# The V product of a step placed behind the third instead of the second chunk of the next step's scores

## Chip, core and metric

One core of a Trainium2 chip runs the whole program. The metric is the device time of one execution in microseconds (us). Engines are named PE (TensorE, matmuls), ACT (ScalarE), DVE (VectorE), POOL (GpSimd) and SP (the queue that issues DMAs).

## What is computed

The input `x` is 4 x 2048 x 256 in fp32. First comes a full attention layer with 16 heads of width 16, then two local-attention and feed-forward layers. The change lies in the first attention, which is this part of the reference, cut to its core:

```python
x = x + attn(layernorm(x))
# attn: per batch (4) and head (16), L = 2048, hd = 16
scores = Q @ K.T / 4 + prior_lambda * gaussian_mask(L)   # 2048 x 2048
attn   = softmax(scores, axis=-1)
out    = attn @ V                                        # 2048 x 16
x = x + (out.transpose(...).reshape(B, L, 256) @ Wo.T + bo)
```

The mask is non-zero only near the diagonal (distance up to 59).

## The kernel before

There are 4 x 16 = 64 heads, and each head is worked in 16 steps of 128 rows, 1024 steps in all. A step `n` is head `n // 16`, key block `kb = n % 16`. The loop runs from `n = -20` to `n = 1024`, because two passes over the scores run 20 steps apart:

- **pass1** (L528) computes 128 queries x 2048 keys in four chunks of 512 columns, each of four matmuls into one of three PSUM banks (`a_b`). DVE takes the row maximum of each chunk, with a plain reduction (L811) or, where the mask reaches into the chunk, with a fused add-and-max (L809), followed by a short read of the accumulator. These maxima are turned into one more row of `q` (rows_T, L573, then ACT and a DMA) for pass2. The step that pass1 works on is 20 ahead of that of pass2.
- **pass2** (L543) computes the scores of 128 keys x 2048 queries, already shifted by the maximum, in four chunks into one of three other PSUM banks (`a_w`). Chunks near the diagonal get up to four small matmuls for the mask as well (L546). ACT takes the exponential of each chunk (L659) into `a_pr`, of which there are four pairs of chunks, so two steps' worth.
- **pv** (L565) is the V product: eight matmuls that multiply the exponentials of one whole step with V and accumulate into `a_po` over the 16 steps of a head. It belongs to the step before: in step `n` the loop calls `pv(n - 1)`. At the end of a head ACT copies `a_po` out (`a_osb`, L692), and the next head's first pv waits for that copy.

pass1 uses the lower 64 rows of the PE array, pass2 the upper 64, pv both halves. A bank is claimed by waiting for the reader of the chunk three before it in the same ring: `claim` waits on `s_free[i]`. In a step without other work pass2's chunk 2 therefore takes the bank that chunk 3 of the step before has left. pv waits for all four exponentials of its step, which is again chunk 3 of the step before.

Between the steps lie "units": projections of q and k (L471), values (L483), transposes of the input (L454), spreading of the softmax sums (L497) and the output projection (L513) of another batch. A table sets at which steps they are called, one per step at most, behind chunk 3. Each unit takes one bank of the `a_w` ring, and ACT copies it out (L620, L629, L641, L642, L649). DVE has side work in some steps as well (statistics for the layer norms, L712 and L784).

Each engine runs its own instruction list in order. The order on PE is the order in which the Python code calls the functions:

```python
for n in range(-LEAD, NS + 1):
    for c in range(4):
        pass1(n, c)
        pass2(n, c)
        if c == 1:
            pv(n - 1)
```

Of the kernel before, what the change touches and what calls it, by code (L numbers as in the profile page):

```python
# [235 lines left out]
def rows_at(n):  # L236

    return (n + LEAD) // W if (n + LEAD) % W == 1 and W < n + LEAD <= NS + 1 else 0
# [69 lines left out]
def attention(nc, S0, x1, a):  # L308
# [118 lines left out]
    def tensor(eng):  # L427
# [91 lines left out]
        def pass1(n, c):  # L519

            g, qb = divmod(n + LEAD, W)
            if g < NB * HA:
                s = g % 3
                bk, full = claim(("rows_of", g, qb, c))
                pe.wait_ge(s_pack[s], PACK * (g // 3 + 1))
                for r in range(4):
                    o = qb * 128 + 32 * r
                    m = eng.matmul(bk[32 * r:32 * r + 32, :], qp[s][0:DEEP, o:o + 32], kp[s][0:DEEP, c * 512:c * 512 + 512], start=True, stop=True)  # L528
                m.then_inc(full, 1)

        def pass2(n, c):

            if not 0 <= n < NS:
                return
            g, kb = divmod(n, W)
            s = g % 3
            pe.wait_ge(s_row[s], ROW * (g // 3 + 1))
            pe.wait_ge(s_setup, 3)
            bk, full = claim(("columns_of", n, c))
            near = [(q, w) for q in range(4) for w in windows(kb * 128 + 32 * q) if w[0] == c]  # L540
            for r in range(4):
                o = kb * 128 + 32 * r
                m = eng.matmul(bk[32 * r:32 * r + 32, :], kp[s][HALF:HALF + DEEP + 2, o:o + 32], qp[s][HALF:HALF + DEEP + 2, c * 512:c * 512 + 512],  # L543
                               start=True, stop=True, skip_group_check=True)
            for q, (_, c0, p0, n_) in near:
                m = eng.matmul(bk[32 * q:32 * q + 32, c0:c0 + n_], sel[HALF:128, :], mt[HALF:128, p0:p0 + n_], start=False, stop=True, skip_group_check=True)  # L546
            m.then_inc(full, 1)

        def pv(n):
            if not 0 <= n < NS:  # L550
                return
            g, kb = divmod(n, W)
            b, h = divmod(g, HA)
            i, k = slot["values", b, 3, 1]
            pe.wait_ge(s_free[i], k)
            pe.wait_ge(s_nh, 3 if b else 2)
            for c in range(4):
                i, k = slot["columns_of", n, c]
                pe.wait_ge(s_free[i], k)
            if kb == 0 and g:  # L560
                pe.wait_ge(s_osb, g)
            for half in range(2):
                rows = slice(HALF * half, HALF * half + HALF)
                for j in range(4):
                    m = eng.matmul(po[32 * j:32 * j + DA + 1, 512 * half:512 * half + 512], v[b % 2][rows, kb, h, :],  # L565
                                   pr[(2 * n + j // 2) % NP][rows, (j % 2) * 512:(j % 2) * 512 + 512], start=kb == 0, stop=kb == W - 1, skip_group_check=True)
            m.then_inc(s_pv, 1)

        def rows_T(what):
            bk, full = claim(what)  # L570
            pe.wait_ge(s_setup, 1)
            pe.wait_ge(s_pk, what[1] + 1)
            eng.transpose(bk.bitcast(F16)[0:32, 0:128], pk[:, :, :].rearrange("p a b -> p (a b)"), identh[:, :]).then_inc(full, 1)  # L573
# [14 lines left out]
        for n in range(-LEAD, NS + 1):  # L588
            for c in range(4):
                pass1(n, c)  # L590
                pass2(n, c)
                if c == 1:
                    pv(n - 1)
            if n in units:
                work[units[n][0]](units[n])
            if rows_at(n):
                rows_T(("rows", rows_at(n) - 1))
# [609 lines left out]
    with nc.Block() as block:  # L1207
        block.tensor(tensor)
        block.scalar(scalar)
        block.vector(vector)  # L1210
        block.gpsimd(gpsimd)
        block.sync(sync)
# [974 lines left out]
```

## Time and profile before

| | |
|---|---|
| median of 3 runs | 5791.14 us (5790.15 to 5794.63) |
| the profiled execution, time | 5793.11 us |
| the profiled execution, span | 5790.9 us |
| mean granted TensorE clock | 0.984 |
| PE busy | 5275.0 us (91%) |
| DVE busy | 4804.4 us (83%) |
| ACT busy | 4306.8 us (74%) |
| POOL busy | 2184.7 us (38%) |

The span is from the first to the last instruction. Shares are means over the whole program, of which the attention with the steps described above is the first 3155 us. PE's busy time is the time in which any matmul is in the array, also a lone one, so it is no measure of how full the array is.

### The profile page before, as it was taken

How to read it: one execution, taken by the hardware profiler on the slowest of the kernel's cores; microseconds unless marked ns; L12 is line 12 of the kernel's file. 1: busy time of each engine (PE TensorE's matmuls, PEld its weight loads, DVE VectorE, ACT ScalarE, POOL GpSimd, SP SyncE). 2: the span in 40 equal slices, each digit the busy share in tenths (PEclk: the TensorE clock that was granted, in tenths of full speed). 3: DMA queues.
4: the chain of work that ended last, by engine and by line, in shares of the span. 5: the costliest groups of instructions: out<-in, count | busy, mean ns of one | idle time of the engine just before them, and what ended most of it. 6: DMA issues, size and time to landing. Idle time of an engine off the chain costs nothing. (4 is left out here: it accounts for less than half of the span.)

```text
span 5790.9 us, 179656 instructions
## 1 busy us (share of the span) xinstructions
PE 5275.0 (91%) x75212; PEld 3174.8 (55%) x75340; DVE 4804.4 (83%) x9925; ACT 4306.8 (74%) x8522; POOL 2184.7 (38%) x1695
## 2 busy tenths in 40 slices
PE   8888888888888888888888999999999999999999
PEld 2333333333333333333332788888888888888787
DVE  5988899888899888999993888888676888888676
ACT  3888888888888888888886677777433677777333
POOL 2011102211013111031001789989111889988222
PEclk7999999999999999999997999999999999999999
DMA  2011101111111111111000454544100444555211
GB/s 83 22 31 37 36 24 35 46 38 35 29 29 44 40 38 33 31 44 46 25 22 12 113 116 111 115 113 112 50 12 6 112 113 113 115 116 113 58 55 48
DMA packets 262970, 343.32 MB, mean 59 GB/s; under 512 B 45664, under 2 KB 165520, under 8 KB 262160
## 3 DMA queue, kind: packets, MB, share of 16 engines
q1 hardware_dynamic: 262160, 331.84, 23.0%
q8 instruction: 592, 9.70, 0.7%
q14 instruction: 218, 1.79, 0.1%
HBM read 104.14 MB, written 33.55 MB: 24 GB/s over the span
## 5 line engine op out<-in xcount | busy, mean ns | idle before, releaser
L659 ACT ACTIVATE a_pr<-a_w,a_expscale 128x512 f32<-128x512 f32 x4096 | 2496.9, 688 | 283.1 <-PE a_w L543 177.9
L811 DVE TENSOR_REDUCE a_mx<-a_b 128x1 f32<-128x512 f32 x2688 | 1729.4, 685 | 235.2 <-PE a_b L528 231.1
L528 PE MATMUL a_b<-a_kp,a_qp 48*32 48x512 f16 x16384 | 1323.9, 384 | 199.3 <-DVE a_mx L809 99.0
L543 PE MATMUL a_w<-a_qp,a_kp 50*32 50x512 f16 x16384 | 1357.6, 385 | 32.3 <-ACT a_pr L659 25.4
L565 PE MATMUL a_po<-a_pr,a_v 64*17 64x512 f32 x16384 | 1143.5, 605 | 191.2 <-ACT a_pr L659 92.2
L528 PEld LDWEIGHTS a_b<-a_kp,a_qp 48*32 48x32 f16 x16384 | 430.9, 92 | 1211.5 <-issue 440.1
L809 DVE CUSTOM_DVE_ANT_0 a_junk<-a_b,a_gw 128x512 bf16<-128x512 f32 x1408 | 966.0, 686 | 144.7 <-PE a_b L528 101.3
L1709 POOL TENSOR_TENSOR l_p<-l_p,l_rc 128x512 f32<-128x512 f32 (+1 forms) x512 | 721.7, 1437 | 29.3 <-DVE l_rc L1607 29.2
L1497 ACT ACTIVATE l_p<-l_S,l_nm 128x256 f32<-128x256 f32 (+1 forms) x1024 | 470.8, 470 | 203.9 <-DVE l_nm L1599 203.9
L1351 PE MATMUL l_G<-l_wqkv,l_hT 128*128 128x512 f32 x2304 | 602.8, 406 | 9.5 <-DVE l_hT L1550 8.2
L543 PEld LDWEIGHTS a_w<-a_qp,a_kp 50*32 50x32 f16 x16384 | 441.6, 92 | 264.1 <-ACT a_pr L659 136.7
L1870 PE MATMUL f_F<-f_hT,f_w 128*128 128x512 f32 x2088 | 509.9, 398 | 1.9 <-DVE f_hT L2005 1.9
L1351 PEld LDWEIGHTS l_G<-l_wqkv,l_hT 128*128 128x128 f32 x2304 | 413.2, 188 | 113.7 <-issue 17.8
L565 PEld LDWEIGHTS a_po<-a_pr,a_v 64*17 64x17 f32 x16384 | 186.5, 92 | 475.6 <-ACT a_pr L659 359.0
L1870 PEld LDWEIGHTS f_F<-f_hT,f_w 128*128 128x128 f32 x2088 | 386.0, 188 | 88.1 <-DVE f_hT L2005 2.7
L954 POOL TENSOR_SCALAR a_r<-a_nm 128x16 f32<-128x16 f32 x64 | 16.5, 258 | 975.1 <-DVE a_nm L817 975.1
L1702 POOL TENSOR_TENSOR l_ri<-l_ss,l_nh 128x16 f32<-128x16 f32 x128 | 372.5, 2910 | 26.3 <-DVE l_ss L1575 20.0
L1948 ACT ACTIVATE f_u<-f_uf 128x512 fp32r<-128x512 f32 x160 | 101.2, 632 | 359.7 <-DVE f_uf L2017 359.7
L936 POOL TENSOR_TENSOR a_heads_sb<-a_osb 128x512 f32<-128x512 f32 x64 | 82.0, 1281 | 749.8 <-ACT a_osb L692 749.8
L1700 POOL TENSOR_TENSOR raw<-raw 128x1024 f32<-128x1024 f32 x128 | 305.5, 2386 | 135.1 <-DVE raw L1565 135.1
L1599 DVE TENSOR_REDUCE l_nm<-l_S 128x2 f32<-128x512 f32 (+1 forms) x512 | 338.4, 661 | 6.0 <-PE l_S L1380 5.5
L1505 ACT ACTIVATE l_pT<-l_R 128x512 f32<-128x512 f32 (+1 forms) x512 | 271.3, 582 | 82.8 <-PE l_R L1392 81.8
(258 smaller groups left out, 8873.0 us busy)
## 6 DMA issues: line engine op xcount, KB each, us to landing
l_qs<-l_qT SPq DMA_DIRECT2D x512, 128.0 KB, 2.3
l_kh<-l_kT SPq DMA_DIRECT2D x512, 128.0 KB, 2.4
l_kl<-l_kT SPq DMA_DIRECT2D x256, 128.0 KB, 2.4
a_qp<-q_parts SPq DMA_DIRECT2D x128, 128.0 KB, 2.8
a_kp<-k_parts SPq DMA_DIRECT2D x128, 128.0 KB, 3.1
l_tab<-in_rotary SPq DMA_DIRECT2D x128, 128.0 KB, 2.4
a_xc<-in_x SPq DMA_DIRECT2D x28, 512.0 KB, 3.8
q_parts<-raw SPq DMA_DIRECT2D x32, 256.0 KB, 2.1
```

Source lines behind the costliest of these rows:

```text
L528: m = eng.matmul(bk[32 * r:32 * r + 32, :], qp[s][0:DEEP, o:o + 32], kp[s][0:DEEP, c * 512:c * 512 + 512], start=True, stop=True)
L543: m = eng.matmul(bk[32 * r:32 * r + 32, :], kp[s][HALF:HALF + DEEP + 2, o:o + 32], qp[s][HALF:HALF + DEEP + 2, c * 512:c * 512 + 512], sta ...
L565: m = eng.matmul(po[32 * j:32 * j + DA + 1, 512 * half:512 * half + 512], v[b % 2][rows, kb, h, :], pr[(2 * n + j // 2) % NP][rows, (j % 2 ...
L659: eng.activation(pr[(2 * n + c // 2) % NP][:, o:o + 512], banks[i], ACT.Exp, scale=expscale[:, :]).then_inc(s_free[i], 1)
L809: t = eng.tensor_tensor_reduce(junk[:, :], banks[i], gw[:, o + WIDE0:o + WIDE0 + 512], 1.0, LOWEST, ALU.add, ALU.max, mx[g % 2][:, qb, c:c ...
L811: t = eng.tensor_reduce(mx[g % 2][:, qb, c:c + 1], banks[i], X, ALU.max)
L1351: m = eng.matmul(G[n % 2][:, :], hT[x][:, c * 128:c * 128 + 128], wq[z][:, c, n * 512:n * 512 + 512], start=i == 0, stop=i == 5)
L1497: y = eng.activation(dst, src, ACT.Exp, bias=nm[t % 2][:, hh:hh + 1], accum_out=sm[t % 2][:, hh:hh + 1])
L1599: eng.tensor_reduce(nm[t % 2][:, 2 * pair:2 * pair + 2], s[:, :].rearrange("p (h k) -> p h k", h=2) if w else z[:, :, 1, :], X, ALU.max, n ...
L1702: eng.tensor_tensor(ri[s][:, :], ss[s][:, :], nh[:, :], ALU.pow).then_inc(s_inv, 1)
L1709: eng.tensor_tensor(z, z, rc[t % 2][:, o:o + 2].unsqueeze(2).to_broadcast([128, 2, 256 if w else 128]), ALU.mult).then_inc(s_norm, 1)
L1870: m = eng.matmul(f[:, :], w1[x][:, c, col * 128:col * 128 + 128], hT[g % 2][z][:, c, :], start=n == 0, stop=n == 5)
```

## The change

One line is changed. In each step the eight matmuls of `pv(n - 1)` are called behind chunk 2 instead of behind chunk 1, on PE alone. Instruction lists of ACT, DVE, POOL and SP are the same as before.

```diff
             for c in range(4):
                 pass1(n, c)
                 pass2(n, c)
-                if c == 1:
+                if c == 2:
                     pv(n - 1)
```

In a step without a unit, this is PE's list before, from chunk 1 to chunk 2 (L528 is pass1, L543 pass2, L565 pv; `a_free0` to `a_free2` are the banks that DVE empties, `a_free3` to `a_free5` those that ACT empties):

```order
L528 MATMUL a_b<-a_kp,a_qp 32x512 [waits a_free1]
L528 MATMUL a_b<-a_kp,a_qp 32x512 x3
L543 MATMUL a_w<-a_qp,a_kp 32x512 [waits a_free5]
L543 MATMUL a_w<-a_qp,a_kp 32x512 x3
L565 MATMUL a_po<-a_pr,a_v 17x512 [waits a_free3]
L565 MATMUL a_po<-a_pr,a_v 17x512 x7
L528 MATMUL a_b<-a_kp,a_qp 32x512 [waits a_free2]
L528 MATMUL a_b<-a_kp,a_qp 32x512 x3
L543 MATMUL a_w<-a_qp,a_kp 32x512 x4
L546 MATMUL a_w<-a_mt,a_sel 32x150 x4
```

And this is the same place after, with chunk 3 behind it:

```order
L528 MATMUL a_b<-a_kp,a_qp 32x512 [waits a_free2]
L528 MATMUL a_b<-a_kp,a_qp 32x512 x3
L543 MATMUL a_w<-a_qp,a_kp 32x512 [waits a_free3]
L543 MATMUL a_w<-a_qp,a_kp 32x512 x3
L546 MATMUL a_w<-a_mt,a_sel 32x150 x4
L565 MATMUL a_po<-a_pr,a_v 17x512 x8
L528 MATMUL a_b<-a_kp,a_qp 32x512 [waits a_free0]
L528 MATMUL a_b<-a_kp,a_qp 32x512 x3
L543 MATMUL a_w<-a_qp,a_kp 32x512 [waits a_free4]
L543 MATMUL a_w<-a_qp,a_kp 32x512 x3
```

The wait for ACT's last exponential of the step before (`a_free3` here) stood on pv, with chunk 2 of both passes behind it; now it stands on pass2's chunk 2, pv follows without a wait of its own, and chunk 3 of both passes lies behind pv.

The second place is the step behind a unit, here the values (L483). Before:

```order
L483 MATMUL a_w<-a_wv,a_hT 32x256 x15
L528 MATMUL a_b<-a_kp,a_qp 32x512 [waits a_free0]
L528 MATMUL a_b<-a_kp,a_qp 32x512 x3
L543 MATMUL a_w<-a_qp,a_kp 32x512 [waits a_free5]
L543 MATMUL a_w<-a_qp,a_kp 32x512 x3
L528 MATMUL a_b<-a_kp,a_qp 32x512 [waits a_free1]
L528 MATMUL a_b<-a_kp,a_qp 32x512 x3
L543 MATMUL a_w<-a_qp,a_kp 32x512 [waits a_free3]
L543 MATMUL a_w<-a_qp,a_kp 32x512 x3
L546 MATMUL a_w<-a_mt,a_sel 32x150 x4
L565 MATMUL a_po<-a_pr,a_v 17x512 x8
```

After, from chunk 1's mask matmuls on:

```order
L546 MATMUL a_w<-a_mt,a_sel 32x150 x4
L528 MATMUL a_b<-a_kp,a_qp 32x512 [waits a_free2]
L528 MATMUL a_b<-a_kp,a_qp 32x512 x3
L543 MATMUL a_w<-a_qp,a_kp 32x512 [waits a_free4]
L543 MATMUL a_w<-a_qp,a_kp 32x512 x3
L565 MATMUL a_po<-a_pr,a_v 17x512 x8
```

Here the bank that pass2's chunk 2 claims is that of the unit, so pv now stands behind ACT's copy of the unit as well.

## Rows read from the trace of the kernel before

**Rows 1.** Busy time by stretch: the steps, the last 15, one short stretch.
```profile
131.20:3098.20 2967.00, 2554.13 (x56179) 948.22 (x56183) 2598.32 (x5689) 2622.13 (x4357) 419.43 (x505) 0.99 0.12 34
3098.20:3155.40 57.20, 54.74 (x537) 13.06 (x528) 0.00 (x0) 36.14 (x59) 0.00 (x0) 0.51 0.02 4
...
2188.00:2190.00 2.00, 2.00 (x40) 0.91 (x28) 0.54 (x1) 1.09 (x3) 2.00 (x2) 0.54 0.00 0
```
The columns are: stretch, its us, busy us of PE, PE's weight load, DVE, ACT and POOL (with instructions), granted TensorE clock, DMA share, GB/s.

**Rows 2.** Waits in 170 to 3110 us: us in total, times, longest.
```profile
ACT a_pr L659 <- PE a_w L543: 168.4, 562, 1.4
ACT a_pr L659 <- PE a_w L546: 94.6, 314, 1.3
...
ACT a_ob L649 <- PE a_w L513: 19.8, 24, 0.8
```

**Rows 3.** Page, costliest groups: busy us, mean ns of one | idle before.
```profile
L659 ACT ACTIVATE a_pr<-a_w,a_expscale 128x512 f32<-128x512 f32 x4096 | 2496.9, 688 | 283.1 <-PE a_w L543 177.9
```

**Rows 4.** Timeline of one plain step: start, us, engine, line, count, idle before.
```profile
1528.99 2.42 ACT L659 ACTIVATE a_pr<-a_w,a_expscale 128x512 f32<-128x512 f32 x4 [0.27 <-PE a_w L543]
...
1530.31 1.08 PE L565 MATMUL a_po<-a_pr,a_v 64*17 64x512 f32 x16
1531.18 0.40 PE L528 MATMUL a_b<-a_kp,a_qp 48*32 48x512 f16 x4
1531.21 0.40 PE L543 MATMUL a_w<-a_qp,a_kp 50*32 50x512 f16 x4
...
1531.62 0.69 DVE L809 CUSTOM_DVE_ANT_0 a_junk<-a_b,a_gw 128x512 bf16<-128x512 f32 x1 [0.19 <-PE a_b L528]
...
1531.68 2.42 ACT L659 ACTIVATE a_pr<-a_w,a_expscale 128x512 f32<-128x512 f32 x4 [0.27 <-PE a_w L543]
...
1532.23 1.88 DVE L811 TENSOR_REDUCE a_mx<-a_b 128x1 f32<-128x512 f32 x3
```

**Rows 5.** Timeline where pass2 stands directly ahead of pv.
```profile
1510.33 0.40 PE L543 MATMUL a_w<-a_qp,a_kp 50*32 50x512 f16 x4 [0.17 <-ACT a_pr L659]
1510.35 1.24 PE L565 MATMUL a_po<-a_pr,a_v 64*17 64x512 f32 x16
...
1511.22 0.40 PE L528 MATMUL a_b<-a_kp,a_qp 48*32 48x512 f16 x4
1511.42 0.39 PE L543 MATMUL a_w<-a_qp,a_kp 50*32 50x512 f16 x4
```

**Rows 6.** Timeline of DVE: two masked chunks, one behind the other.
```profile
1581.34 0.69 DVE L809 CUSTOM_DVE_ANT_0 a_junk<-a_b,a_gw 128x512 bf16<-128x512 f32 x1 [0.19 <-PE a_b L528]
...
1582.18 0.69 DVE L809 CUSTOM_DVE_ANT_0 a_junk<-a_b,a_gw 128x512 bf16<-128x512 f32 x1
```

**Rows 7.** Timeline of ACT around a long unit: an output projection, a k projection.
```profile
1701.86 2.42 ACT L659 ACTIVATE a_pr<-a_w,a_expscale 128x512 f32<-128x512 f32 x4 [0.27 <-PE a_w L543]
...
1707.11 3.62 ACT L659 ACTIVATE a_pr<-a_w,a_expscale 128x512 f32<-128x512 f32 x6
...
2147.02 2.42 ACT L659 ACTIVATE a_pr<-a_w,a_expscale 128x512 f32<-128x512 f32 x4 [0.27 <-PE a_w L543]
...
2153.11 3.57 ACT L659 ACTIVATE a_pr<-a_w,a_expscale 128x512 f32<-128x512 f32 x6
```

**Rows 8.** Timeline of ACT and DVE at a head's end.
```profile
1561.59 1.26 ACT L659 ACTIVATE a_pr<-a_w,a_expscale 128x512 f32<-128x512 f32 x2 [0.27 <-PE a_w L543]
1562.74 1.02 ACT L692 ACTIVATE a_osb<-a_po 128x1024 f32<-128x1024 f32 x1
...
1565.22 1.89 DVE L811 TENSOR_REDUCE a_mx<-a_b 128x1 f32<-128x512 f32 x3 [1.20 <-PE a_b L528]
...
1607.08 1.02 ACT L692 ACTIVATE a_osb<-a_po 128x1024 f32<-128x1024 f32 x1
```

**Rows 9.** Timeline of ACT in the last head.
```profile
3109.41 2.42 ACT L659 ACTIVATE a_pr<-a_w,a_expscale 128x512 f32<-128x512 f32 x4 [1.30 <-PE a_w L543]
```

## Prediction, made before the changed kernel ran

> **What bounds the kernel now.** I read first the busy time by stretch, to see what the change can reach. The steps run from 131 to 3098 us; in these 2967 us DVE is busy 2598 and ACT 2622, so neither is full, and the granted clock is 0.99, the 2.4 GHz level. The last 15 steps, without pass1, run at 0.51, the 1.2 GHz level [rows 1]. Behind 3155 us nothing is touched.
>
> Then the waits. ACT waits 562 + 314 = 876 times for a pass2 chunk, 263 us, about 0.30 us each [rows 2]. The timeline of one step shows where. ACT starts four exponentials at 1528.99, and the next four at 1531.68: a period of 2.69. Four in a row take 2.42, one alone takes 0.69 [rows 3], so they start (2.42 - 0.69)/3 = 0.58 apart and ACT alone could do a step in 2.31. The four in a row are chunks 2 and 3 of step n-1, then chunks 0 and 1 of step n. Call T the end of chunk 3's exponential: 1528.99 + 0.58 + 0.69 = 1530.26. pv starts at T + 0.05, pass1's chunk 2 at T + 0.92, pass2's at T + 0.95, and the exponential of chunk 2 at T + 1.42, that is 0.47 after its matmuls. ACT had run out of chunks 0 and 1 before that [rows 4]. So pv's 0.87 us lies between the end of one step's exponentials and the third chunk of the next. DVE waits for the same pv: it gets chunk 2 at 1531.62, 0.44 after the matmuls, having waited 0.19 [rows 4].
>
> **What the change does to a plain step.** Nothing is added or removed, the eight matmuls move behind chunk 2, so the cost is all in who waits for whom.
>
> pass2's chunk 2 now starts at T + 0.05, where pv started, and its exponential can run at T + 0.52, while ACT wants it only at T - 0.11 + 2 x 0.58 = T + 1.05. Hidden, with 0.5 to spare. pv comes behind it. Where a row transposition has shifted the ring, the old kernel already has pass2 ahead of pv: pass2 at 1510.33, pv at 1510.35, then pass1 at 1511.22 and pass2 at 1511.42 [rows 5]. So pv starts its lower half at once and its upper half about 0.2 later; pass1's chunk 3 comes 0.89, pass2's 1.09 behind the first pass2. Taken over: pass1's chunk 3 at T + 0.94, pass2's at T + 1.14, exponential at T + 1.61. ACT wants chunk 3 at T + 1.62. It just fits, so PE and ACT together could turn a step in about 2.31 instead of 2.69. With mask matmuls in chunk 2 or 3 I add up to 0.1.
>
> The Trainium skill bears on this spot (TensorE: Matmul & The Clock Gate, section The mechanism): matmuls start and end in program order, and weights are loaded beside running matmuls only where the row group differs. Read strictly, pv's upper half could not be prepared under pass2's chunk 2, and all of pv would lie 0.2 later; the row agrees for the upper half and not for the lower. By the strict reading chunk 3 would be 0.2 late in each plain step, the first rival below.
>
> Next DVE. Three plain reductions in a row take 1.88, so (1.88 - 0.69)/2 = 0.60 from one to the next, and a masked chunk is 0.61 ahead of the next start (1531.62 to 1532.23) [rows 4]. A masked one behind a masked one starts 0.84 later [rows 6]. The mask reaches 22 of a head's 64 chunks, and 7 of them stand ahead of another masked one, counted from the code. A head costs DVE 42 x 0.60 + 15 x 0.61 + 7 x 0.84 = 40.2 us, or 2.51 a step. **DVE becomes the bound**: 2.51 against ACT's 2.31. PE does not hold it back: from one chunk-3 reduction to the next the path through pass1's chunk 2, pv and pass1's chunk 3 is 0.69 + 0.05 + 0.22 + 0.87 + 0.44 = 2.27, under 2.41. Today a plain head takes 1607.08 - 1562.74 = 44.34 [rows 8].
>
> **What is not won.** (a) At a head's end the first pv waits for ACT's copy of a_po. ACT starts chunk 3 at 1561.59 + 0.58 = 1562.17; the copy ends at 1563.76, so pv is 0.9 later than otherwise, and today DVE idles 1.20 there [rows 8]. Afterwards chunk 2 is ahead of it, and of that idle I work out 2.95 - 2.41 = 0.54 if DVE comes to it without lag (pv at 1.64, chunk 3's matmuls at 2.51, its reduction at 2.95, counted from ACT's start of chunk 3), about 0.5: 62 x 0.5 = 31 us. (b) Long units. There are four rows of 24 waits (the one shown, and the like for values, q and k projections), 96 in all [rows 2]. With PE busy on the unit, two steps take, from chunk 3's start to chunk 3's start, (1707.11 + 1.73) - (1701.86 + 0.58) = 6.40 for 48 of them and (2153.11 + 1.73) - (2147.02 + 0.58) = 7.24 for the 48 projections [rows 7]. PE and ACT set these, not the place of pv: pv moves behind ACT's copy of the unit, but chunk 3 is still ready when ACT gets there. I cost them at no change. DVE idles in them by 6.40 - 5.03 and 7.24 - 5.03, together 66 + 106 = 172 us, which also hides its statistics. (c) Mask matmuls and small misfits between the engines: 0.25 a head, 15 us.
>
> **The sum.** pass1 runs in 1004 steps, 62.75 heads, from 131 to about 3084 (3098 less five steps of 2.69). Afterwards: 62.75 x 40.2 = 2523, + 172 + 31 + 15 = 2741 us, against 2953: 212 less. The five steps left at full clock win 0.38 each (2 us). The last 15: a step is now 2.42 + 1.30 = 3.72 [rows 9]; pv at half clock (1.74) still bounds them, and putting one pass2 chunk (0.43) ahead and one exponential less behind saves 0.58 - 0.43 = 0.15 each (2 us). In all 216. As a second way: 22 plain heads win 44.34 - 40.9 = 3.4 each (75), and the 876 - 352 = 524 other waits about 0.24 each (126): 201. I take 209, between the two. The profiled execution took 5793.1, 2 over the median, so 5584 by it and 5582 by the median.
>
> **Rivals.**
> - The forecast, DVE becomes the bound and about 209 us go: 0.66, its own range 5545 to 5630.
> - The wait moves to chunk 3. It fits by 0.01 only. If all of pv runs behind pass2's chunk 2 and the masks, chunk 3 is 0.2 to 0.3 late, ACT's step is 2.5 to 2.6, and added to DVE's uneven load some 0.12 of each of 812 plain steps is lost: 5582 + 97 = 5680. For it: no slack. Against: the overlap in [rows 5]. 0.19.
> - DVE's load fits better between the waits than I think (its reductions slide into the long units), so nearly all of ACT's 263 us go: 5791 - 263 = 5528. 0.07.
> - No change, because another wait steps in at once in full: the row of maxima or the loads of q and k, whose times in us stay while the steps shrink. They would have to take all of the 0.17 a step. Nothing on PE waits for them now. 0.03.
> - Slower: the clock. PE must stay at 2.4 GHz in the steps. It fell to 0.54 at 2188, where PE had waited for a copy of a_po [rows 1], and in the last head a step at 0.51 takes 3.72 [rows 9]. A plain step in that state costs at least 3.72 - 2.51 = 1.2 more, so from 209/1.2 = 174 such steps on the kernel is slower; with 300 it would be 5582 + 360 = 5942. Against: PE's pauses get shorter and one chunk more is worked in the pause at a head's end. 0.05. The Trainium skill describes this case (TensorE: Matmul & The Clock Gate, A second HAM failure mode: psum-queue depth-cycling): a PE that pauses briefly between groups while it goes round its PSUM banks can swing between the two levels. The row of the steps, 0.99 with the same pauses, does not show it.
>
> **How the numbers follow.** Predicted is the likeliest, 5582. The range runs from 5535 to 5685: it takes in the forecast's own and most of the second, and ends just above the third. About 0.2% (12 us) is what a measurement tells from no change. Faster: 0.66 + 0.19 + 0.07 = 0.92; same 0.03; slower 0.05.
>
> **What would show it.** ACT's 263 us of waits for L543 and L546 fall under 120; what remains for it stands on chunk 3. DVE's waits fall from 369 idle to about 180, and it is over 93% busy in the steps. A plain head takes about 40.9. PE's waits for DVE grow. Pairs of steps with a long unit stay at 6.4 and 7.2. Wrong it would be if ACT waits 0.2 at chunk 3 in each step, if DVE's spacing of 0.60 grows when PE and ACT are fuller, or if the clock of the steps drops under 0.97.

## The result

| | before | changed |
|---|---|---|
| median | 5790.65 us (5783.14 to 5794.63, 4 runs) | 5565.25 us (5561.30 to 5567.32, 4 runs) |
| profiled execution | 5793.11 us | 5561.30 us |
| span | 5790.9 us | 5559.5 us |
| mean granted TensorE clock | 0.984 | 0.991 |

The changed kernel takes 0.9611 of the time of the kernel before (95% interval 0.9595 to 0.9628): 225 us less by the medians. The forecast was 5582 us, range 5535 to 5685.

Where the time went is read from ACT's copies of `a_po` (L692), one at the end of each of the 64 heads. The profiled spans differ by 231.4 us:

| stretch | before | changed | less |
|---|---|---|---|
| up to the copy of the first head | 178.1 | 171.9 | 6.2 |
| 19 heads with no unit in them ("plain heads" below), each | 44.35 | 40.43 | 3.92 (74.5 in all) |
| the 43 others up to the 63rd copy | 2075.0 | 1944.6 | 130.4 |
| the last head | 58.66 | 37.24 | 21.4 |
| all behind | 2636.5 | 2637.6 | -1.1 |

Three more heads have no unit in them either; they win 3.5 to 4.4 us each and are counted with the 43, of which 40 have units.

These are the stretches and the waits in the trace of the changed kernel. First, the busy time of the steps and of the last head (columns as in [rows 1]):

```profile
131.20:2884.60 2753.40, 2495.86 (x56119) 944.75 (x56103) 2537.21 (x5684) 2580.77 (x4349) 417.56 (x503) 1.00 0.13 36
2885.00:2922.00 37.00, 32.73 (x556) 9.60 (x552) 0.00 (x0) 35.68 (x62) 1.28 (x1) 1.00 0.03 6
```

DVE is idle for 216 us of the steps now, against 369 before [rows 1]. The last head ran at a clock of 0.51 before; now it is at 1.00, the 2.4 GHz level, and ACT is busy in nearly all of it.

The clock changed in the steps ahead of it as well. Between the first copy of `a_po` and the last head the trace of the kernel before has nine short stretches at the lower level, of which that at 2188 [rows 1] is one. Eight of the nine begin within 2 us behind the start of a head's copy, during or just behind PE's pause for it. The changed kernel has one such stretch, at 327, and none at a head's end. Here are two more of the kernel before, and the one of the changed kernel:

```profile
608.00:610.00 2.00, 2.00 (x39) 0.68 (x20) 0.72 (x2) 1.08 (x3) 1.74 (x2) 0.50 0.04 11
1373.00:1375.00 2.00, 2.00 (x40) 0.62 (x28) 0.23 (x1) 0.67 (x2) 1.80 (x2) 0.50 0.01 2
```

```profile
327.00:329.00 2.00, 2.00 (x37) 0.49 (x25) 1.36 (x4) 0.89 (x3) 2.00 (x3) 0.50 0.00 0
```

Next, the waits in 170 to 2870 us (us in total, times, longest):

```profile
ACT a_pr L659 <- PE a_w L543: 31.5, 130, 0.8
ACT a_v L629 <- PE a_w L483: 28.2, 24, 1.2
ACT a_tmp L641 <- PE a_w L471: 28.1, 24, 1.2
ACT a_ob L649 <- PE a_w L513: 28.0, 24, 1.2
ACT raw L641 <- PE a_w L471: 27.2, 24, 1.2
ACT a_pr L659 <- PE a_w L546: 12.1, 39, 1.7
...
DVE a_mx L811 <- PE a_b L528: 102.2, 131, 1.5
DVE a_junk L809 <- PE a_b L528: 35.4, 36, 1.7
```

ACT's 876 waits for a chunk of pass2, 263 us [rows 2], are 169 waits and 44 us. They stood on chunk 2 (873 of the 876); all 169 that are left stand on chunk 3. Its waits for the long units have grown, from 19.8 us in 24 waits [rows 2] to about 28 in each of the four groups. The timeline of plain steps (columns as in [rows 4]) shows the new order of things:

```profile
798.94 7.23 ACT L659 ACTIVATE a_pr<-a_w,a_expscale 128x512 f32<-128x512 f32 x12 [0.23 <-PE a_w L543]
799.02 0.08 DVE L809 DVE_READ_ACCUMULATOR2_ANT a_mx<- 128x1 f32 x1
799.02 1.88 DVE L811 TENSOR_REDUCE a_mx<-a_b 128x1 f32<-128x512 f32 x3
...
799.76 0.40 PE L528 MATMUL a_b<-a_kp,a_qp 48*32 48x512 f16 x4
799.77 0.40 PE L543 MATMUL a_w<-a_qp,a_kp 50*32 50x512 f16 x4
799.99 1.04 PE L565 MATMUL a_po<-a_pr,a_v 64*17 64x512 f32 x16
800.82 0.68 DVE L809 CUSTOM_DVE_ANT_0 a_junk<-a_b,a_gw 128x512 bf16<-128x512 f32 x1
800.85 0.39 PE L528 MATMUL a_b<-a_kp,a_qp 48*32 48x512 f16 x4
800.86 0.39 PE L543 MATMUL a_w<-a_qp,a_kp 50*32 50x512 f16 x4
...
801.42 1.88 DVE L811 TENSOR_REDUCE a_mx<-a_b 128x1 f32<-128x512 f32 x3
```

DVE goes from 799.02 to 801.42 without a gap, a step of 2.40. Chunk 2 of both passes (799.76) now stands ahead of pv (799.99), chunk 3 (800.85) behind it, and ACT works through twelve exponentials with no wait. What is left of DVE's idle time in a plain head is at the head's end, where [rows 8] had 1.20:

```profile
826.96 1.02 ACT L692 ACTIVATE a_osb<-a_po 128x1024 f32<-128x1024 f32 x1
...
829.43 0.69 DVE L811 TENSOR_REDUCE a_mx<-a_b 128x1 f32<-128x512 f32 x1 [0.24 <-PE a_b L528]
```

### The profile page after: what moved, and what is told of

It reads as the page before. It is cut to its first block and busy times, and to the rows that moved or that the text cites. A ratio compares the mean times of both kernels' runs of the same rounds, so it can differ in the third digit from the quotient of the medians.

```text
span 5559.5 us, 179608 instructions
## 1 busy us (share of the span) xinstructions
PE 5193.5 (93%) x75212; PEld 3169.5 (57%) x75340; DVE 4744.1 (85%) x9925; ACT 4269.2 (77%) x8522; POOL 2185.2 (39%) x1695
## 5 line engine op out<-in xcount | busy, mean ns | idle before, releaser
L659 ACT ACTIVATE a_pr<-a_w,a_expscale 128x512 f32<-128x512 f32 x4096 | 2455.6, 698 | 59.6 <-PE a_w L543 33.7
L811 DVE TENSOR_REDUCE a_mx<-a_b 128x1 f32<-128x512 f32 x2688 | 1705.3, 683 | 124.1 <-PE a_b L528 117.3
L528 PE MATMUL a_b<-a_kp,a_qp 48*32 48x512 f16 x16384 | 1424.1, 383 | 197.8 <-DVE a_mx L809 92.4
L543 PE MATMUL a_w<-a_qp,a_kp 50*32 50x512 f16 x16384 | 1459.4, 383 | 51.7 <-ACT raw L642 39.0
L565 PE MATMUL a_po<-a_pr,a_v 64*17 64x512 f32 x16384 | 1165.1, 591 | 21.5 <-ACT a_osb L692 20.6
L528 PEld LDWEIGHTS a_b<-a_kp,a_qp 48*32 48x32 f16 x16384 | 403.2, 90 | 1272.4 <-DVE a_mx L811 627.0
L543 PEld LDWEIGHTS a_w<-a_qp,a_kp 50*32 50x32 f16 x16384 | 413.8, 90 | 284.5 <-ACT a_pr L659 117.7
L565 PEld LDWEIGHTS a_po<-a_pr,a_v 64*17 64x17 f32 x16384 | 282.2, 93 | 96.8 <-ACT a_osb L692 38.8
```

The costliest lines, as they stand in the source:

```text
L659: eng.activation(pr[(2 * n + c // 2) % NP][:, o:o + 512], banks[i], ACT.Exp, scale=expscale[:, :]).then_inc(s_free[i], 1)
L811: t = eng.tensor_reduce(mx[g % 2][:, qb, c:c + 1], banks[i], X, ALU.max)
```

## The experiments

**Theory**: the V product lay between ACT's last exponential of a step and the third chunk of the next; behind chunk 2 it is covered, and DVE's work on the maxima is the bound. **Rivals**: ACT, or PE's chain through chunk 3, is the new bound; and, for the last head, the low clock is given and only a shorter chain counts. All medians below stand beside runs of the kernel before on the same chip, whose medians lie at 5789 to 5792 us. The changed kernel itself was not run again beside them, so a difference from its 5565 us can be off by some 2 us.

### Two scratch tiles for the masked maxima

A masked chunk on DVE writes a scratch tile `junk` and waits for the masked chunk before it. With two tiles it waits for the one before that, which is long done. The second tile lies on constants that are no longer used; the lines that declare it are left out here.

```diff
-                if junk_of:
-                    dve.wait_ge(*junk_of.pop())
+                if len(junk_of) > 1:
+                    dve.wait_ge(*junk_of[-2])
                 junk_of.append((s_free[i], k))
-                t = eng.tensor_tensor_reduce(junk[:, :], ...
+                t = eng.tensor_tensor_reduce(junks[len(junk_of) % 2], ...
```

On the changed kernel:

> The changed kernel, with two scratch tiles for the masked maxima instead of one, so that a masked chunk behind a masked one need not wait 0.23 us for it. If DVE bounds the changed kernel, a head's floor on DVE falls by 7 x 0.23 = 1.6 us; ACT and PE then come near (38.1 and about 39 a head), so I expect plain heads at 39.0 to 39.6 instead of 40.4 and 5565 - 55 = 5510 (5490 to 5530). Rival: ACT or the PE chain through chunk 3 is the bound (ACT's exponentials run 0.607 apart without a gap); then nothing changes, 5565 within 8.

5506.07 us (5504.17 to 5508.52), ratio 0.9506 (0.9493 to 0.9519) to the kernel before: 59 us below the changed kernel. Plain heads take 39.28 us. The timeline of DVE in this kernel shows the second masked chunk 0.61 behind the first, where [rows 6] has 0.84:

```profile
781.08 0.68 DVE L810 CUSTOM_DVE_ANT_0 a_junk<-a_b,a_gw 128x512 bf16<-128x512 f32 x1
781.69 0.09 DVE L810 DVE_READ_ACCUMULATOR2_ANT a_mx<- 128x1 f32 x1
781.69 0.69 DVE L810 CUSTOM_DVE_ANT_0 a_ones_gt<-a_b,a_gw 128x512 bf16<-128x512 f32 x1
782.30 0.09 DVE L810 DVE_READ_ACCUMULATOR2_ANT a_mx<- 128x1 f32 x1
```

On the kernel before:

> The kernel before, with the same two scratch tiles. If the V product behind chunk 1 bounds it, DVE's pairs lie beside that wait, plain heads stay at 44.35 and the time within 8 us of 5791. If DVE had a share in the old bound, it is faster by up to 1.6 us a head, 5700.

5789.47 us (10 runs, 5786.08 to 5793.62), ratio 0.9997 (0.9988 to 1.0006), plain heads 44.36. The same edit on DVE is worth nothing while pv stands behind chunk 1 and 59 us once it stands behind chunk 2. So DVE was not the bound before and is after. The plain heads win 1.15 us each of the 1.6 by which DVE's floor fell: from 40.43 to 39.28, with the floor now at 40.2 - 1.6 = 38.6. What takes the remaining 0.4 was not traced.

### Pass2's chunk 2 worked twice

The four matmuls of pass2's chunk 2 are issued twice, the second time over the first, which adds 0.22 us of PE time in each step and leaves the output as it is.

```diff
-            for r in range(4):
+            for r in list(range(4)) * (2 if c == 2 else 1):
```

> The kernel before, with pass2's four matmuls of chunk 2 issued twice in each step (0.22 us of PE time more, same output). If chunk 2 behind the V product is on the chain that sets ACT's pace, each of some 812 plain steps grows by 0.22: 5791 + 178 = 5969. If PE has slack there, nothing changes.

5982.90 us (two runs), ratio 1.0333 (1.0313 to 1.0354): 192 us more, and plain heads at 47.5 instead of 44.35, 0.20 a step. Chunk 2 behind pv was on the chain.

> The changed kernel, with the same doubling. Chunk 2 itself is wanted 0.5 us after it is ready, but the V product and chunk 3 stand behind it. My forecast has ACT's chunk 3 just in time for a step of 2.31 and DVE at 2.51, so of 0.22 us the first 0.2 should be swallowed: 5565 + 10 to + 60 (5575 to 5625). If chunk 3 were already on the chain, all of it comes through: 5565 + 178 = 5743. If PE had ample slack: 5565.

5676.96 us (5669.03 to 5683.12), ratio 0.9804 (0.9789 to 0.9819): 112 us over the changed kernel, a miss. The plain heads did what was expected: 41.62 against 40.43, 0.07 a step out of 0.22. The remainder lies in the 43 other heads, 2026.8 against 1944.6, 82 us or 1.9 a head. I had left out the steps with a long unit and behind one, where PE is the bound. From one chunk 3 on ACT to the one two steps on, the 96 pairs of such steps grew by 0.30 to 0.42 us out of 0.44 added, 32 us in all; each other step by 0.07, 812 x 0.07 = 57. Together 89 of 112; the remainder was not traced. Chunk 2 itself is off the chain, and by this run PE has some 0.15 us of slack in a plain step and little around long units.

### The V product behind chunk 3

```diff
-                if c == 2:
+                if c == 3:
                     pv(n - 1)
```

> The V product behind chunk 3. If DVE bounds the changed kernel, the plain heads stay at 40.2 to 40.4; the rest of DVE's idle time at a head's end (0.24) goes, as chunk 3 no longer waits for ACT's copy, and pairs with a long unit may get back 0.1 to 0.3: 5545 to 5565. Rival: the V product now stands ahead of the next step's chunks 0 and 1 and ACT waits there: over 5600.

5632.09 us (5621.51 to 5642.62), ratio 0.9727 (0.9711 to 0.9744), slower than behind chunk 2. The plain heads stay at 40.57, which was expected. The loss lies in the other 43 heads, 2000.2 against 1944.6. Its waits on ACT:

```profile
ACT a_tmp L641 <- PE a_w L471: 40.7, 24, 1.8
ACT a_v L629 <- PE a_w L483: 40.3, 24, 2.0
ACT raw L641 <- PE a_w L471: 38.3, 24, 1.8
ACT a_ob L649 <- PE a_w L513: 36.1, 24, 1.5
```

The unit stands behind pv on PE, and the later pv is, the longer ACT waits for the unit: 0.84, 1.16 and 1.62 us for the three places. In two of the four runs the clock of the last head fell as well (the mean clock reads 0.985 and 0.986 in the slower two, 0.990 and 0.991 in the faster).

### The place of the V product around long units

First with the old place in the steps behind a long unit (`long` is `units[n - 1][0] in HOLDS`, and then `c == 1`):

> The changed kernel, but in the 96 or so steps behind a long unit the V product stays behind chunk 1. I costed these steps at no change; then this kernel is at 5565 within 8. If the move costs time there (the pairs of steps read 6.5 and 7.55 in the trace of the changed kernel against 6.4 and 7.24 before), it is up to 48 x 0.11 + 48 x 0.31 = 20 us faster: 5545. If the move gains there: slower than 5573.

5567.19 us (5564.92 to 5569.00), ratio 0.9616 (0.9600 to 0.9632): no difference. Then, on the kernel with two scratch tiles, with the old place in the steps that hold the unit:

```diff
+                long = n in units and units[n][0] in HOLDS
-                if c == 2:
+                if c == (1 if long else 2):
                     pv(n - 1)
```

> The kernel with two scratch tiles (5506 us), and the V product back behind chunk 1 in the steps that hold a long unit themselves. In the changed kernel ACT waits 1.15 us for each of the 96 long units instead of 0.84, 31 us more in all. If that comes from chunk 3 and the unit standing behind the V product in the unit's own step, the waits go back towards 0.84 and the time falls by 10 to 30 us: 5476 to 5496. If PE is the bound in these steps wherever the V product stands, nothing changes: 5506 within 8. If DVE loses there what it gains (chunk 2 is late again): slower, 5515 to 5530.

5507.88 us (5506.62 to 5508.98), ratio 0.9509 (0.9493 to 0.9525) against 0.9506: no difference. The waits of this kernel say why:

```profile
ACT a_pr L661 <- PE a_w L547: 22.4, 76, 1.7
ACT a_v L631 <- PE a_w L484: 20.9, 24, 1.1
...
ACT a_pr L661 <- PE a_w L544: 16.7, 59, 0.8
```

ACT's waits for the units are back at 0.84 each, and its waits for chunks of pass2 have grown from 14 to 39 us in exchange. The wait was moved, not removed. A pair of steps with a long unit, from chunk 3 to chunk 3 on ACT, takes 6.42 us (output projections), 6.59 (values) and 7.44 (projections) in the kernel with two scratch tiles, and 6.47, 6.59 and 7.44 here: PE's work sets the pair, wherever pv stands in it.

### The last head and its clock

The kernel before, with the new place only in the last 15 steps (from the third of the last head on):

```diff
-                if c == 1:
+                if c == (2 if n > NS - W + 1 else 1):
                     pv(n - 1)
```

> The kernel before, with the V product behind chunk 2 only in the last head (15 steps). My forecast costed this part at 2 us, because it took the 1.2 GHz level of that head as given. The trace of the changed kernel shows the head at 1.00 and 21 us shorter. If the place of the V product in these steps alone keeps the clock up, this kernel has a granted clock near 1.00 in the last head and is about 21 us faster than the kernel before (5770). Rival: the clock is kept up by what went before (fuller heads); then the head stays at 0.5 and the gain is 2 us (5789).

5792.53 us (11 runs, 5783.61 to 5794.73), ratio 0.9998 (0.9989 to 1.0006). The first theory fell. In its last head:

```profile
3096.50:3100.00 3.50, 2.03 (x38) 0.75 (x36) 0.00 (x0) 3.17 (x6) 1.27 (x1) 1.00 0.00 0
3100.00:3104.00 4.00, 3.82 (x50) 1.16 (x54) 0.00 (x0) 2.88 (x6) 0.00 (x0) 0.51 0.18 39
3104.00:3120.00 16.00, 16.00 (x174) 4.42 (x168) 0.00 (x0) 11.24 (x19) 0.00 (x0) 0.50 0.00 1
```

And the other way round (`1 if n > NS - W + 1 else 2`):

> The changed kernel, with the V product back behind chunk 1 in the last head only. By the first theory the clock falls to 0.5 there and the time is 19 to 21 us over that of the changed kernel (about 5585). By the rival (what went before decides) the clock stays and only the plain loss of 15 x 0.36 = 5 us comes back (5570).

5571.32 us (5566.99 to 5574.11), ratio 0.9620 (0.9607 to 0.9633). The clock stays at 1.00 with pv at the old place, and the head takes 42.23, 5 us more than with the new one. So the same last 15 steps run at either level, and what decides lies ahead of them. Just ahead is the step in which pv of the new head waits for the copy of `a_po`. PE's pause there is 1.19 us in the kernel before, and 0.52 in this experiment, as in the changed kernel, since a chunk is worked first. The rows are one of the kernel before and one of this experiment:

```profile
3096.91 1.08 PE L565 MATMUL a_po<-a_pr,a_v 64*17 64x512 f32 x16 [1.19 <-ACT a_osb L692]
```

```profile
2887.09 1.08 PE L565 MATMUL a_po<-a_pr,a_v 64*17 64x512 f32 x16 [0.52 <-ACT a_osb L692]
```

So that single step was changed alone, in both directions (`n == NS - W + 1` in place of `n > NS - W + 1`):

> The kernel before, with the V product behind chunk 2 in one single step: the second of the last head, in which PE pauses for ACT's copy of a_po. The place in the 14 steps behind it did not matter (clock 0.50 with the new place there, 1.00 with the old one). If this one step with its pause decides whether the clock falls, the last head is 42.2 us long at a clock of 1.00 and the kernel 16 us faster than before: 5775. Rival: what matters lies further back (how full the heads with pass1 are), then the last head stays at 58 us and the time at 5791.

> The changed kernel, with the V product behind chunk 1 in that one step only. If the step decides: the clock falls to 0.50 and the last head takes 56 us instead of 37, 5565 + 19 = 5584. Rival, further back: 37.5 us and 5565.

Both came out mixed. The kernel before with the new place in that step: 5770 to 5795 us, five of ten runs at 5770 to 5779 with a mean clock of 0.989 or 0.990, five at 5784 to 5795 with 0.983 to 0.986; ratio 0.9986 (0.9975 to 0.9997). The changed kernel with the old place there: 5564.22 and 5564.51 us at 0.991 and 0.990, 5581.76 and 5586.66 at 0.986 and 0.985; ratio 0.9625 (0.9605 to 0.9645). The profiled execution is one in which it fell:

```profile
2888.59 1.08 PE L565 MATMUL a_po<-a_pr,a_v 64*17 64x512 f32 x16 [1.19 <-ACT a_osb L692]
```

```profile
2887.00:2891.00 4.00, 2.53 (x44) 0.85 (x40) 0.00 (x0) 3.67 (x6) 1.28 (x1) 1.00 0.00 0
2891.00:2895.00 4.00, 3.82 (x50) 1.22 (x54) 0.00 (x0) 2.88 (x6) 0.00 (x0) 0.54 0.16 35
```

In these runs the one step moves the odds to about half, in either kernel (five of ten and two of four, a small count); it does not decide alone. The last try fills PE instead: the kernel before, with pass2's chunks 0 and 1 worked twice in the last head (`2 if c < 2 and n >= NS - W else 1`).

> The kernel before, with pass2's matmuls of chunks 0 and 1 issued twice in the last head (16 steps, same output), which fills PE where it would idle. If a fuller PE in the last head keeps the clock up, the head takes about 43 us at 1.00: 5775. If the clock falls all the same, the doubled matmuls cost at half clock: 58.7 + up to 16 x 0.86 = 72 us, 5791 to 5805.

5797.05 us (10 runs, 5776.79 to 5804.38), ratio 1.0003 (0.9992 to 1.0015). In seven runs the clock fell (0.983 to 0.985) and the doubled matmuls were paid at half clock; three, at 0.988 or 0.989, took 5777 to 5782. More work in the last head helps some runs and not most.

One earlier run bears on this too: the kernel before with pass2's chunk 2 worked twice in every step. Its pv is at the old place, and its pause ahead of the last head is 1.19 us as in the kernel before. Yet the clock stays up through the last head, which takes 46.60 us; its two runs, 5982.99 and 5982.81 us, agree. These are its pause and its last head:

```profile
3297.77 1.08 PE L565 MATMUL a_po<-a_pr,a_v 64*17 64x512 f32 x16 [1.19 <-ACT a_osb L692]
```

```profile
3297.00:3341.00 44.00, 35.54 (x600) 11.78 (x600) 0.00 (x0) 36.81 (x61) 1.29 (x1) 1.00 0.02 5
```

So a pause of 1.19 us does not always bring the fall. The 62 earlier heads' ends of the kernel before say the same: PE's pause there is 1.00 to 1.19 us, and 1.86 at three of them, and the eight short falls include these three and five with 1.19. In the changed kernel no such pause is over 0.52 us, and there is no fall.

## Why the prediction was right, and where it was not

**What bounded the kernel.** Right. Doubling chunk 2 cost the kernel before 0.20 us a step and the changed one 0.07 in its plain heads.

**Chunk 3 just in time.** Right. In the last head, where DVE has nothing to do, 60 exponentials run without a wait. This is the row of ACT in the changed kernel:

```profile
2885.59 35.02 ACT L659 ACTIVATE a_pr<-a_w,a_expscale 128x512 f32<-128x512 f32 x60
```

That is (35.02 - 0.69)/59 = 0.58 each, 2.33 a step against the 2.31 worked out. There is no pass1 in that head. Where pass1 runs too, ACT reaches the same pace when it has been held up, as behind the end of a head at 1587 in the changed kernel, (4.73 - 0.69)/7 = 0.58:

```profile
1587.70 4.73 ACT L659 ACTIVATE a_pr<-a_w,a_expscale 128x512 f32<-128x512 f32 x8
```

The strict reading, in which all of pv starts 0.2 late and chunk 3 with it, came half true. In the last head pv starts with pass2's chunk 2, and the next chunk of pass2 comes 1.08 behind:

```profile
2888.11 0.40 PE L543 MATMUL a_w<-a_qp,a_kp 50*32 50x512 f16 x4 [0.18 <-ACT a_pr L659]
2888.12 1.24 PE L565 MATMUL a_po<-a_pr,a_v 64*17 64x512 f32 x16
2889.19 0.60 PE L543 MATMUL a_w<-a_qp,a_kp 50*32 50x512 f16 x8
```

In a step with pass1, whose chunk 2 starts in the lower rows at the same moment, all of pv does start 0.22 late (799.77 and 799.99 above). But pass2's chunk 3 still comes 1.09 behind its chunk 2 (800.86), as forecast; only pass1's chunk 3 comes 1.09 behind instead of 0.89. The rule of the Trainium skill (TensorE: Matmul & The Clock Gate, The mechanism) does not say what the strict reading made of it: the lower half of pv is in another row group than pass2, and by the rule its weights may be loaded at once. These rows tell when the matmuls start, not which load held them, so whether the rule was at work is not shown.

**DVE becomes the bound.** Right, and shown by the scratch tiles: no gain before, 59 us after. Its floor of 40.2 us a head met 40.43 measured. I had added 0.7 to the floor for a plain head, 40.9: the idle time at the head's end is 0.24 and not 0.5, and masks and misfits cost next to nothing (40.2 + 0.24 = 40.44). That is 0.5 us for each plain head, 9 for 19. Why the idle time is half of what I worked out was not tested; probably DVE comes there with some chunks in hand.

**Long units at no change.** Right. Over all 96 of them, two steps take 6.49 us (output projections), 6.63 (values) and 7.48 (projections) before, and 6.42, 6.68 and 7.51 after, and the two experiments that moved pv back around them made no difference. ACT's waits for the units did grow, by 31 us in all, but inside the pair: the step that holds an output projection went from 2.71 to 2.32 us, and the one behind it from 3.79 to 4.11. The prices taken, 6.40 and 7.24 from one unit each, were at the low end; with the means the term is 192 us and not 172.

**The sum for the steps.** 209 us were taken. Up to the 63rd copy the kernel is 211 us shorter (74.5 + 130.4 + 6.2). That it fits to 2 us is in part luck, as errors of this size stand against each other: the heads' ends cost some 15 us instead of 31 and the misfits of plain heads next to nothing instead of 15, while the long units cost 20 more, and the 40 heads with units some 14 beyond that. And not all of the 211 comes from the chain. The short falls of the clock at heads' ends, which the sum did not have, cost about 1 us each: the head behind 2188 takes 47.92 us in the kernel before and 47.03 in the run with the new place in one single step, whose trace has no fall there. The eight together are some 8 us, an estimate, and the changed kernel has none of them.

**The last 15 steps.** Wrong in size: 2 us forecast, 21.4 measured, nearly all of what separates 5582 from 5565. The term took the 1.2 GHz level of the old trace as given, and asked only what a shorter chain saves at that level; the kernel before with the new place in the last head shows that this part is real but small (56.56 against 58.66). What counts is that the clock no longer falls: the same steps with pv at the old place take 42.23 at full clock against 58.66 at half, 16 us, and the new place takes 5 more off. I had treated the clock as a danger to the change only, while the row at 2188 [rows 1], half clock behind a wait for the same copy, also said that a shorter pause could win.

Why the clock stays is shown in part: the step with the pause moves the odds, and so does something ahead of it that is different in the two kernels. With the new place in all steps of the heads before and in that step, it stayed up, by the mean clock of 0.989 to 0.991, in all 17 runs of the four such kernels (the changed kernel, the one with the old place in the last head, the one with two scratch tiles, the one with the old place behind long units); in the kernel before, and in it with the new place in the last head, it fell in each run listed (0.983 to 0.986). But with the old place everywhere and chunk 2 worked twice it did not fall in the last head either. 

What the other part is, the fuller heads before or the moment at which the last head begins, stays open; neither was tried alone. The run with chunk 2 worked twice speaks against the length of the pause as the whole cause, and does not tell these two apart.

**The rivals.** That ACT or chunk 3 would bind fell with the scratch tiles. That nearly all of ACT's 263 us would go was close for ACT, of which 44 are left, but not for the time, since DVE set the pace of ACT: its exponentials run 0.60 apart instead of 0.58 and show no gap. The clock did not fall more in the steps but less: 1.00 with one short fall, against 0.99 with nine. The prediction took the 0.99 as a sign that there were no swings between the levels; there were these nine.

**The signs.** ACT's waits for pass2 fell to 44 us (forecast under 120), and all that remain stand on chunk 3, as forecast. DVE is busy for 92% of the steps, with 216 us idle, short of the 93% and 180 forecast. The waits of PE's weight loads of pass1 for DVE grew, from 678 us (367.1 and 310.8) to 1050 (596.6 and 453.8). Pairs with a long unit stayed.

**The fastest version** that was run is the changed kernel with two scratch tiles: 5506 us, 0.9506 of the kernel before.

## What to carry to other kernels

Where two consumers with rings of banks hang on one in-order producer, look for the item in the producer's list that lies between the release of a bank and the next chunk, and put it at the place where the consumers hold the most finished chunks; then count the floor of each consumer, since the next bound takes part of the gain (here 2.51 us a step against 2.31). An edit that is worth nothing before can be worth 1% afterwards, so try the small ones again once the bound has moved. And do not price a stretch at a low clock by its old clock: ask what PE did just ahead of the fall, and whether the change touches that.

## What the runs showed of the hardware that was not expected

- Whether TensorE's clock falls in a stretch can differ from execution to execution of one program. With one step of 1024 changed, ten runs of one kernel spread over 25 us, with a mean clock of 0.983 to 0.990, where the kernel before spreads over 9 to 12. The Trainium skill (TensorE: Matmul & The Clock Gate, What's actually happening) says of the rise at the start of a kernel that its point varies from run to run. These runs show the other direction in mid-kernel: the fall itself may come or stay away.
- The level does not follow from the work alone: the same last 15 steps, with the same instructions in the same order, run at 0.50 in the kernel before (58.66 us for the head) and at 1.00 in the changed kernel with the old place in the last head (42.23 us).
- Pauses of PE of 1.19 us at a head's end were followed by a short fall in some cases of the kernel before and not in most; all three of 1.86 us were, and none of the changed kernel's, of 0.52 us at most. In the steps with pass1 the clock came back within a few us; in the last head, with less work in each step, it stayed down to the head's end.
- Two masked maxima on DVE with a semaphore between them start 0.84 us apart, and 0.61 without the wait: 0.23 us less, with a second tile to write to and so no wait on the engine's own last result.
